# The last four batches of a two-adapter linear layer in two levels of a seven-product scheme, the first four in one

## What is computed

```python
# x: (8, 512, 2048), all float32
# first adapter (rank 16, one of 8 per batch)
x = x + einsum('bnr,bor->bno', einsum('bni,bri->bnr', x, B0[ids0]), A0[ids0])
# second layer: a full matrix W (2048 x 2048) and an adapter (rank 16, one of 16 per batch)
base = einsum('bsi,io->bso', x, W)
lora = einsum('bsr,bro->bso', einsum('bsi,bir->bsr', x, A1[ids1]), B1[ids1])
y = x + base + lora
```

## Time and profile before

| what | value |
|---|---|
| profiled execution | 1402.34 us, of it span 1400.7 us |
| instructions in the span | 15653 |
| TensorE (matmul) busy | 1367.2 us, 6016 matmuls |
| VectorE / ScalarE / GpSimd busy | 810.2 / 405.9 / 165.0 us |
| DMA | 261.81 MB, of it read from HBM 213.52, written 48.30 |
| clock of TensorE, mean of the span | 0.993 of full |

### The profile page before, as it was taken

One profiled execution on the slowest core, in us unless ns is written; L12 is line 12 of the kernel. 1 busy time (PEld: TensorE's weight loads), 2 busy tenths in 40 slices (PEclk: granted clock), 3 DMA queues, 4 the chain that ended last, 5 costly groups with the idle time before them and its releaser, 6 DMA issues.

```text
span 1400.7 us, 15653 instructions
## 1 busy us (share of the span) xinstructions
PE 1367.2 (98%) x6016; PEld 1129.2 (81%) x6016; DVE 810.2 (58%) x941; ACT 405.9 (29%) x462; POOL 165.0 (12%) x317
## 2 busy tenths in 40 slices
PE   5999999999999999999999999999999999999997
PEld 4888888888878888888887888888887888888886
DVE  3455855357776455646775555555766445554675
ACT  2332222223234223322332323232322422232230
POOL 3200100111123010012011010012012001001202
PEclk8999999999999999999999999999999999999999
DMA  8864843458887343357684252446785334234755
GB/s 303 310 225 134 299 158 113 153 186 280 294 280 240 122 136 120 129 195 246 236 289 146 86 173 96 151 151 213 256 297 187 99 120 135 91 91 133 223 201 180
DMA packets 76778, 261.81 MB, mean 187 GB/s; under 512 B 12176, under 2 KB 12176, under 8 KB 76576
## 3 DMA queue, kind: packets, MB, share of 16 engines
q1 hardware_dynamic: 57600, 205.55, 43.5%
q0 software_dynamic: 19104, 55.27, 11.7%
HBM read 213.52 MB, written 48.30 MB: 187 GB/s over the span
## 4 chain that ended last, share of the span: by engine, by line
PE 85%; DVE 5%; DMA 5%; ACT 2%; issue 2%; POOL 0%; POOLq 0%; SPq 0%; ACTq 0%; DVEq 0%
PE y_ps L1024 76%; PE lr_ps L955 4%; PE p_ps L997 3%; DMA w_raw<-in_W 2%; PE y_ps L976 2%; ACT w_hi L555 2%; DVE w_lo L708 1%; DVE w_raw L694 1%; DVE b_lo L721 1%; DMA w_raw<-w_sum 1%; DVE u L776 1%; DMA stage_all<-lrw 0%; DMA u<-in_A0n 0%; DVE u L777 0%; DVE val L835 0%
## 5 line engine op out<-in xcount | busy, mean ns | idle before, releaser
L1024 PE MATMUL y_ps<-b_hi,w_hi 128*128 128x512 f32 x1792 | 699.3, 390 | 15.3 <-DVE w_lo L708 8.8
L1024 PE MATMUL y_ps<-b_lo,w_hi 128*128 128x512 f32 x1792 | 698.6, 390 | 0.0
L1024 PE MATMUL y_ps<-b_hi,w_lo 128*128 128x512 f32 x1792 | 698.4, 390 | 0.0
L708 DVE TENSOR_TENSOR w_lo<-w_raw,w_hi 128x1024 fp32r<-128x1024 f32 x216 | 264.6, 1225 | 460.9 <-ACT w_hi L555 460.9
L555 ACT CAST w_hi<-w_raw 128x1024 fp32r<-128x1024 f32 x216 | 227.6, 1054 | 879.5 <-PE y_ps L1024 474.9
L1024 PEld LDWEIGHTS y_ps<-b_hi,w_hi 128*128 128x128 f32 x1792 | 337.3, 188 | 86.6 <-DVE w_lo L708 8.8
L1024 PEld LDWEIGHTS y_ps<-b_hi,w_lo 128*128 128x128 f32 x1792 | 337.2, 188 | 70.2
L1024 PEld LDWEIGHTS y_ps<-b_lo,w_hi 128*128 128x128 f32 x1792 | 337.3, 188 | 70.1
L721 DVE TENSOR_TENSOR b_lo<-x_raw,b_hi 128x1024 fp32r<-128x1024 f32 x112 | 136.5, 1219 | 0.0
L566 ACT CAST b_hi<-x_raw 128x1024 fp32r<-128x1024 f32 x112 | 117.5, 1049 | 2.4 <-DMA x_raw<-in_xT 2.4
L694 DVE TENSOR_TENSOR w_raw<-w_raw 128x1024 f32<-128x1024 f32 x64 | 78.1, 1221 | 19.5 <-DMA w_raw<-in_W 11.6
(11 more groups left out here) (81 smaller groups left out, 605.8 us busy)
## 6 DMA issues: line engine op xcount, KB each, us to landing
w_raw<-in_W SPq DMA_DIRECT2D x208, 512.0 KB, 3.8
w_raw<-w_sum SPq DMA_DIRECT2D x96, 512.0 KB, 3.6
x_raw<-in_xT SPq DMA_DIRECT2D x64, 512.0 KB, 5.4
out_y<-u POOLq DMA_DIRECT2D x64, 256.0 KB, 6.4
out_y<-stage_all POOLq DMA_DIRECT2D x64, 256.0 KB, 3.4
lr_raw<-lrw POOLq DMA_DIRECT2D x64, 128.0 KB, 4.0
w_sum<-w_raw SPq DMA_DIRECT2D x8, 512.0 KB, 6.2
c_kept<-stage_all POOLq DMA_DIRECT2D x16, 256.0 KB, 3.2
```

Source lines behind the costliest of these rows:

```text
L708: dve.tensor_tensor(w_lo[n % 2][:, :, :], w_tile(n)[:, :, :], w_hi[n % 2][:, :, :].bitcast(F32), ALU.subtract).then_inc(w_ready, 1)
L1024: last = pe.matmul(bank[:, :], w[n % 2][:, c, t * P:(t + 1) * P], x[:, 2 * j + c, :], start=(j == 0 and c == 0 and w is w_hi and x is b_hi ...
```

## The change

The first part (`one_level`) is the old kernel for batches 0 to 3, with `PAIRS = NB // 4`: two pairs. The second part (`two_level`) does batches 4 to 7 at once. Its outer level has the two feature halves and, as column blocks, the pairs (4, 5) and (6, 7): outer products M1, M2, M7, M6, M4, M3, M5. Each of them is a 1024 x 1024 by 1024 x 1024 product (two batches wide), solved by the same scheme once more, with quarters of 512 and single batches: inner products Q1, Q2, Q6, Q5, Q7, Q3, Q4. So there are 49 products of 512 x 512 by 512 x 512, each 4 output tiles by 4 chunks by 3 passes, 48 matmuls in two half products; `n` counts the 98 half products, 14 to an outer product, and "M6 u2" is the half product 2 of M6. Q1, Q6, Q7 and Q4 accumulate in the same four PSUM banks, one on top of the other, and are read out (128x1024, two banks at once) after each; Q2, Q5 and Q3 use two other banks in turn.

What else is new:

- The first part's pair 0 also makes F3 and F5, the sums of W for P3 and P5, and keeps them in HBM (`store_kept`, SP, 16 stores of 512 KB; the tiles stand in the place of X21, whose load for pair 1 moves to P1 of pair 1). Pair 1 loads them ready-made, as one block a unit.
- The inner level's four sums of W, for each of the seven outer products, are made in 14 jobs during the first part: a job loads four tiles of 512 KB (rows of 1 KB in HBM), makes four sums of 128x1024 on VectorE, and stores four tiles into `w_ops` from GpSimd's queue. Ten jobs begin at (0, P3, u2) and every six units after it, two more at (1, P7, u2) and (1, P4, u2), and two at (1, P4, u2) and (1, P3, u2), so that three begin at (1, P4, u2).
- The second part reads two halves of 512 KB of W per product and splits both W (128x1024) and x (128x1024) in every half product. The outer level's sums of x are made per batch: `first_diff` (two sums of 128x1024, one operand through `tmp` buffers loaded by SP) and `x_diff` (one of 128x2048). M7's and M6's x are kept in HBM for later use.
- The evictions that begin an output are copies on ScalarE in M1, M7, M4 and M5, all others are additions on VectorE.
- Output: M2 and M7 write their results to y directly. M6, M4 and M5 add theirs onto y in HBM by accumulating DMAs (`accum_op=ALU.add`), 32 of 512 KB, and eight more add the adapters' part of the first outputs (`store_fix`, from two buffers `fix_tile` that ScalarE fills). `fin` (VectorE, M5) adds what M3 and M5 left in SBUF.
- The adapters' output matmuls go into the product's own bank where they can, or to a bank of their own, from which VectorE adds them (`lr_add`) to `stage` or `uq`.
- Layouts of x, W and y in HBM are grouped by two or four chunks of 128 features; a store of y is 512 KB (256 KB in the first part).
- Before the first part ends, `early(n)` starts the second part's first loads and splits.

```diff
...
-    PAIRS = NB // 2
+    PAIRS = NB // 4
...
-        return o in (P3, P5) or (p, o) == (0, P6)
+        return p == 0 and o in (P6, P3, P5)
...
+M1, M2, M7, M6, M4, M3, M5 = range(7)
+Q1, Q2, Q6, Q5, Q7, Q3, Q4 = range(7)
+Q_UNITS = 14
...
+ADDS = {Q1: ((C11, True),), Q2: ((C11, False),), Q6: ((C12, True),), Q5: ((C12, False), (C22, True)),
+        Q7: ((C22, False),), Q3: ((C12, False),), Q4: ((C21, True),)}
...
+W_BLOCK = {M1: A11, M2: A12, M4: A22}
+W_SUM = {M7: S3, M6: S2, M3: F3, M5: F5}
...
+    halves = [(o, h) for o in (M2, M1, M7, M6, M4, M3, M5) for h in range(2)]
+    jobs = [(*halves[i], 0, unit(0, P3, 2) + 6 * i) for i in range(10)]
+    jobs += [(*halves[10 + i], 1, unit(1, P7, 2) + 8 * i) for i in range(2)]
+    jobs += [(*halves[12 + i], 2, unit(1, P4, 2) + 8 * i) for i in range(2)]
...
+    job_loads, job_sums, job_stores = {}, {}, {}
+    for i, (_, _, s, n) in enumerate(jobs):
+        for t, late in ((tc, 0), (td, 0), (ta, 1 if s == 0 else 0), (tb, 4 if s == 0 else 0)):
+            job_loads.setdefault(n + late, []).append((i, t))
+        for k, late in ((js3, 2), (js1, 2), (js2, 3), (js4, 5 if s == 0 else 3)):
+            job_sums.setdefault(n + late, []).append((i, k))
...
+        def store_kept(n):
+            use = keep_use(n)
+            sp.wait_ge(presum_done, presums.index(n) + 1)
+            sp.dma_start(unit_of(w_sum[F5 if use >= UNITS else F3], use % UNITS), w_tile(n)
+                         ).then_inc(f_stored[use % 4], 16)
...
+        def job_sum(i, k):
+            o, h, s, _ = jobs[i]
+            a, c, d, b = (job_use(i, t)[0] for t in (ta, tc, td, tb))
+            if k == js3:
+                dve.wait_ge(*job_loaded_for(i, ta))
+                dve.wait_ge(*job_loaded_for(i, tc))
+                if o in (M1, M4):
...
+    def late_sums(n):
+        if not 0 <= n < LAST:
+            return []
+        mo, u = at(n)
+        out = []
+        if mo < M5:
+            for v, i in ((8, 0), (10, 2), (12, 3)):
+                if u == v and x_worked(mo + 1, i):
+                    out.append(("xq", mo + 1, i))
+            if u == 13:
+                out.append(("t3", mo + 1))
+        if n == 0:
+            out.append(("t3", M1))
+        if u == 1:
+            out.append(("t2", mo))
+        if u == 2:
+            out.append(("t4", mo))
+        return out
...
+    def evicts(n, part):
+        if part == 0:
+            n -= 1
+        if not 0 <= n < LAST:
+            return []
+        po = n % Q_UNITS // 2
+        q, h = n // 2, n % 2
+        if po in CHAIN:
+            return [(q, 2 * h, 2, c, begins) for c, begins in ADDS[po]] if part == 0 else []
...
+    def by_act(q, begins):
+        return begins and product(q)[0] in (M1, M7, M4, M5)
...
+        def store_stage(mo, c, h):
+            g, m = GROUP[mo][c], 4 * (c // 2) + 2 * h
+            one_pair, other = batch(0, c % 2), batch(1, c % 2)
+            tiles, stored = stage[:, g, 2 * h:2 * h + 2, :], stage_stored[g][h]
+            pool.wait_ge(*quarter_done(mo, c, 2 * h + 1))
+            if mo == M2:
+                pool.dma_start(y_at(one_pair, m), tiles).then_inc(stored, 16)
+            elif mo == M7:
+                pool.dma_start(y_at(other, m + 8), tiles).then_inc(stored, 16)
+                pool.dma_start(y_at(one_pair, m + 8), tiles).then_inc(stored, 16)
+            else:
+                pool.wait_ge(u_stored[c], 16 * 4)
+                pool.dma_start(y_at(other if mo == M5 else one_pair, m + 8), tiles, accum_op=ALU.add
+                               ).then_inc(stored, 16)
...
+        def store_u2(c, h):
+            m = 4 * (c // 2) + 2 * h + 8
+            pool.wait_ge(*quarter_done(M6, c, 2 * h + 1))
+            pool.wait_ge(stage_stored[GROUP[M7][c]][h], 16 * stage_stores(M7, c, h))
+            for pair in (1, 0):
+                pool.dma_start(y_at(batch(pair, c % 2), m), uq[:, c, 2 * h:2 * h + 2, :], accum_op=ALU.add
+                               ).then_inc(u_stored[c], 16)
...
+        def lr_copy(s):
+            f, t = fix_at[lr_tiles[s][3], lr_tiles[s][4] // 2 * 2], lr_tiles[s][4] % 2
+            act.wait_ge(lr_mm_done, s + 1)
+            if t == 0:
+                if f >= SLOTS:
+                    act.wait_ge(fix_stored[f % SLOTS], 16 * (f // SLOTS))
...
+            early, rest = second.vector(dve)
+            first.vector(dve, early)
+            rest()
+        @block.tensor
+        def _(pe):
+            first.tensor(pe)
+            second.tensor(pe)()
...
+                        for i, (w, b) in enumerate(((w_hi, b_hi), (w_hi, b_lo), (w_lo, b_hi))):
+                            last = pe.matmul(out, w[:, h, c, col:col + P], b[x],
+                                             start=(po in (Q1, Q2, Q5, Q3) and c == 0 and i == 0),
+                                             stop=(c == 3 and i == 2), skip_group_check=po in CHAIN or mo in (M4, M5))
+                    last.then_inc(tile_done, 1)
```

More of the change, by code:

```diff
@@ L150, in lora_residual_program, with job_counts @@
+    job_no = {use: v + 1 for v, use in enumerate(use for n in sorted(job_sums) for use in job_sums[n])}
+    def job_counts(table, tile_of):
+        counts, out = {}, {}
+        for n in sorted(table):
+            for i, what in table[n]:
+                tile = job_tile(jobs[i][2], tile_of(what))
+                counts[tile] = counts.get(tile, 0) + 1
+                out[i, what] = counts[tile]
+        return out
+    job_store_no = job_counts(job_stores, lambda k: JOB_SUM[k])
     plain = [n for n in range(LAST) if n % 4 != 3 or finds_p(n) or adds_lr(*at(n)[:2])]
@@ new lines, in lr_w_free, with w_tile, y_at @@
+    def lr_w_free(i):
+        p, b, half, _ = lr_plan[i]
+        if p == 0 and b == 0:
+            return fix_mm_done, UNITS * (half + 1)
+        return tile_done, tile(p, {(0, 0): P2, (0, 1): P4, (1, 0): P3, (1, 1): P5}[b, half], 7) + 1
+    def w_tile(n):
+        if n // UNITS == P6:
+            return s2[n % 2]
+        if keep_use(n) is not None:
+            j = keep_use(n) % 4
+            return x_raw[X21][:, 2 * j:2 * j + 2, :]
+        return w_raw[main_raw(n)]
+    def y_at(b, m):
+        return yT[(b * C + m) // 2, :, m % 2, :]
@@ new lines, in sum_kept, with job_use, job_loaded_for @@
+    def sum_kept(kind, u):
+        if kind == S3:
+            k = raw_of[u] + 1
+            return w_stored[k % RAWS], 16 * s3_stores[k]
+        if kind == S2:
+            return s2_stored[u % 2], 16 * (u // 2 + 1)
+        return f_stored[u % 4], 16 * ((UNITS * (kind == F5) + u) // 4 + 1)
+    def job_use(i, t):
+        s, t = job_tile(jobs[i][2], t)
+        return job[s][t], s, t
+    def job_loaded_for(i, t):
+        s = jobs[i][2]
+        before = [v for v in range(i) if jobs[v][2] == s]
+        return job_loaded[s], 64 * len(before) + (48 if s == 0 and t != tb else 64)
@@ new lines, in job_stored_of, with job_tile_free @@
+    def job_stored_of(i, k):
+        _, s, place = job_use(i, JOB_SUM[k])
+        return job_stored[s][place], 16 * job_store_no[i, k]
+    def job_tile_free(i, t):
+        o, h, s, _ = jobs[i]
+        if s == 0 and t == tb:
+            return [(job_summed, job_no[i, js2]), job_stored_of(i, js3)]
+        before = [v for v in range(i) if jobs[v][2] == s]
+        if before:
+            k = js4 if s == 0 and t == ta else next(k for k, tile in JOB_SUM.items() if tile == t)
+            return [(job_summed, job_no[before[-1], js4]), job_stored_of(before[-1], k)]
+        if s == 0:
+            return [unit_end(unit(0, P4, 7)), (p_added, 6)]
+        return [(x_ready, 4 * (PRODUCTS + (P7 if s == 1 else P4)) + 4)]
@@ L1073 @@
         "B0": b0.reshape(-1, r, c, P).transpose(0, 3, 2, 1),
[L1075 removed]
+        "W": w.reshape(2, 2, 4, P, 2, 2, n).transpose(4, 0, 5, 1, 3, 2, 6).reshape(4, 4, P, 4, n),
         "A1": a1.reshape(-1, c, P, r).transpose(0, 2, 1, 3),
```

2554 lines of the change are left out of this document (1771 added, 783 removed).

## The result

The changed kernel takes 1451.64 us (median of four runs, 1450.26 to 1452.12) against 1403.99 (1402.41 to 1405.49), ratio 1.0345, 95% interval 1.0326 to 1.0365: **47.7 us slower**, where 1351 was forecast. The profiled execution took 1451.56 us, span 1449.9.

The account below looks back on a forecast made before the run. TensorE's matmul count was taken as the bound: 1325.0 us with additions hidden, plus 8 (first-part DMA), 8 (VectorE), 4 (M6 DMA), 3 (ends), 1.5 (clock) makes 1349.5; the run median lies 1.5 above, so 1351, range 1330 to 1388.

Parts of the forecast that it names:

- Matmuls removed: Batches 4 to 7: 332 fewer matmuls (2556 for 2888) at 226.3 ns, 75.1 us saved, all on TensorE's path.
- Durations of VectorE: Assumed operation times: 1.22 us for 1024 columns or a pair of PSUM tiles, 2.3 us for sums of 2048 columns.
- M6 beyond 100 us: Sign that the forecast is wrong and B or C holds: M6 taking over 100 us, where 81 us was reckoned.
- The DMA engines, first part: P3, P5 of pair 0 and P1 of pair 1: added transfers outrun 400 GB/s, costing 8 us (0 to 38).
- its excess of 2 us lies in the same slack: P4 of pair 1 asks 417 GB/s; its 2 us excess is absorbed by W being loaded two units ahead.
- VectorE waits: TensorE waits for late VectorE: about 1 us in M6, 3 in M5, 4 at P4 of pair 1; 8 together (0 to 25).
- M6's accumulating DMA: Accumulating stores in M6 may pass their bytes twice, but most have no waiter nearby: 4 us (0 to 37).
- The exception that was made: Stores with a waiter nearby: the two fix buffers, which ScalarE needs again two corrections later; adapter loads behind them also counted.
- Clock: After a few TensorE waits, matmuls run briefly at the 1.2 GHz level: 1.5 us added.
- A: Rival: all additions are hidden behind the matmuls, 1331 us; chance 0.23.
- B: Rival: DMA bounds both stretches, at 337 GB/s and two passages per accumulating store, 1403 us, at best 1385; chance 0.14.
- C: Rival: accumulating stores pass one after another, 12.8 us each, M6 taking 269 us in place of 81, 1540 us; chance 0.09.

## Why the prediction was wrong

Taken out one by one, in this order, the costs end at the base: 1451.6 - 60.7 (jobs) - 28.6 (adding) - 9.0 (kept sums) - 2.9 (order) = 1350.4. The forecast of 1351 stood where the change would be with nearly all its transfers left out, and that the two agree is chance: the forecast is 1331 with everything hidden and 20 us for all that is not, the emptied kernel (all four out) is 1331 and 19 us, nearly all of it waits for VectorE in M6 and M5 and the clock behind them.

The same account for the forecast, each cost with the clock lost behind it: the first part's transfers 53.0 (jobs 44.0, kept sums 9.0) where 8 stood, VectorE 39.0 (job sums 14.9 and 1.8 with the transfers, 2.9 and 19.4 in M6 and M5) where 8 stood, the adding 28.6 where 4 stood. That is 120.6 in place of 20.

- **Matmuls removed, 75.1 us:** right (x5684, 311 in 70 us). Durations of VectorE were right as well (2285 ns for 2048 columns, 1223 for a pair of PSUM tiles), and so were the places of most waits: P5 of pair 0, P1 and P4 of pair 1, M6, M5. Not foreseen was P3 of pair 1 (7.9 us at 751 us). M6 beyond 100 us, one of the signs of being wrong, came true: 107.3.
- **The DMA engines, first part, 8 us (0 to 38):** the term that failed most, with 44.0 for the jobs' transfers and 9.0 for the kept sums. Two errors. The rate was read off two stretches of 5 and 10 us; the third of these rows, 297 GB/s at a share of 0.84 over 45 us, makes 354 at full share. After the change, over 140 us of full share, the engines moved 352 GB/s:

```profile
DMA packets 18671, 49.24 MB, mean 352 GB/s; under 512 B 1933, under 2 KB 7733, under 8 KB 18664
```

  At 352 my own sum reads 65.3 MB / 352 = 185.5, less 145 and 11, 29 us in place of 8, an estimate. The Trainium skill (DMA: Bandwidth & Descriptors, Bandwidth) has about 358 GB/s per core for the HBM side; the first part agrees, but M6 and M4 of the changed kernel with plain stores have slices of 400 to 424 GB/s (1120 to 1190 us in 40 slices), so here it is no ceiling:

```profile
GB/s 229 309 300 257 145 358 421 405 417 408 390 413 401 418 413 419 422 413 330 394 395 408 419 413 423 411 423 424 274 318 328 255 158 124 289 148 276 213 122 225
```

  And the term stopped at P4 of pair 1, "its excess of 2 us lies in the same slack": there a late job load, six job sums and the split stand one behind the other (13.2 us). By products, the transfers alone lose 28 us from P3 of pair 0 to P1 of pair 1 against the kernel without jobs, and 14 in P3 of pair 1. With the 9.0 of the kept sums the first stretch lost some 37 us, 8 more than the rate explains; the 14 lie where the term had nothing.
- **VectorE waits, 8 us (0 to 25):** mis-sized as well, 39 and beyond the range. For the job sums 14.9 where I had 4, and late loads are not the reason, since these were measured without loads. M5 lost 16 us in the trace where 3 stood: a wait of 4.6 for `val`, two before and one after it, and the clock behind them. M6 lost some 11 where 1 stood, with plain stores and without jobs too: waits of 3.8 and 2.2 us and the clock behind them. Where the count of lateness went wrong is open; it had no cost for the clock, and that is part of it.
- **M6's accumulating DMA, 4 us (0 to 37):** mis-sized; 26 to 29, of them 15 in M6, 9 in M4 and 2 in M5 with the jobs in place. The two passages were worked out (18 or 37 us) and then argued away, because few stores have a waiter. But loads share the engines with them. The exception that was made, ScalarE's wait for a fix buffer, cost TensorE nothing. In the last 70 us of the hole (queue: packets, MB, share):

```profile
q0 software_dynamic: 2823, 9.31, 65.8%
q1 hardware_dynamic: 4873, 9.43, 39.4%
```

  The stores' queue held two thirds of the engines, and all of SyncE's transfers, the loads of W that TensorE needs among them, moved at 135 GB/s.
- **Clock, 1.5 us:** mis-sized; some 30, already inside the costs above. Behind the wait of 13.16 us the matmuls lie 0.42 us apart, the 1.2 GHz level, as the earlier trace rows show it once, and the three dear windows have a mean clock of 0.89 to 0.92. The 30 us are added up from the starts of the matmuls; no run takes the clock out by itself.
- **Rivals:** A (1331) is 19 us below even the emptied kernel. B had the mechanism, both stretches bound by the DMA engines, and its "two passages"; it came to 1403, 15 us short in the first part, 3 in the adding and 31 in VectorE's waits. C (stores one after another) is not what happened: accumulating stores in M6 took 6 to 25 us to land, but up to eight were in flight, and from 1131 to 1163 us eleven of them landed.

Open: why full engines move 352 GB/s in the first part and over 400 elsewhere (not the 1 KB rows: with long ones it was 349), and why the waits in M6 and M5 that are left in the emptied kernel are longer than worked out. M6 takes 91.0 us and M5 97.7 there, where 81 and 84 of TensorE's time stood; some 8 us of the difference are clock, by the same count as above.

## What to carry to other kernels

Price a transfer that you add at the rate of the longest full stretch in the trace, stage by stage, and take no "nobody waits for it" as a price of zero: it delays the loads that somebody does wait for. Count an accumulating DMA's bytes twice. And where an engine's order is fixed, put a helper's work that waits for its own load behind what the bound engine needs (argued from the hole at P4; no run here moved the job sums behind the splits), since a wait is paid again in the clock: here 85 us more of waits brought some 30 us more lost at the lower level.

## What the runs showed of the hardware

- An accumulating store from GpSimd: its issue is recorded with 1.14 to 1.43 us in the kernel before (0.55 for a plain one), though in a row they start 0.6 to 1.0 us apart; 9.3 us to land 256 KB (6.4), and the engines' time of a second passage, 308 and 316 GB/s for the extra bytes.
- Job loads in rows of 1 KB or 4 KB: the same time (ratios 1.0347 and 1.0345), though the share fell a little (630 to 770 us 0.84 against 0.86).
- The two DMA queues don't share the engines by need: in the 70 us up to 1190, 512 KB of W from HBM took 34.2 us (median of 4) beside accumulating stores, and 16.2 in the same 70 us of the changed kernel with plain ones.
